# Experts: the activation evaluated twice on ScalarE, into a half-precision and a single-precision buffer, instead of once with a cast on VectorE

## The reference, cut to what matters

```
t = _ln_t(tokens)                       # 6272 tokens of 256 channels
gate_logits = t @ Wg + bg
top_w, top_i = top_k(gate_logits, 2)    # softmax over the two
for e in range(8):
    h = gelu(t @ W1[e] + b1[e])         # 256 -> 1024
    out = out + w_dense[:, e:e + 1] * (h @ W2[e] + b2[e])   # 1024 -> 256
```

## Time and profile before

| | |
|---|---|
| median of three timed runs | 1256.61 us (1252.85 to 1258.9) |
| profiled execution, span | 1258.3 us, mean granted TensorE clock 0.952 |
| TensorE matmuls busy | 1111.1 us, 88% |
| VectorE busy | 880.8 us, 70% |
| ScalarE busy | 621.6 us, 49% |
| GpSimd busy | 727.7 us, 58% |
| experts' activations on ScalarE | 392 of 128x256 and 64 of 128x128 |
| experts' casts and subtractions on VectorE | 424 each, 327 and 461 ns in the mean |

### The profile page before, as it was taken

One profiled execution on the slowest core, in us unless ns is written; L12 is line 12 of the kernel. 1 busy time (PEld: TensorE's weight loads), 2 busy tenths in 40 slices (PEclk: granted clock), 3 DMA queues, 4 the chain that ended last, 5 costly groups with the idle time before them and its releaser, 6 DMA issues. The chain is left out here.

```text
span 1258.3 us, 37927 instructions
## 1 busy us (share of the span) xinstructions
PE 1111.1 (88%) x12025; PEld 947.3 (75%) x12026; DVE 880.8 (70%) x3115; ACT 621.6 (49%) x1315; POOL 727.7 (58%) x786
## 2 busy tenths in 40 slices
PE   4898888989989879972399999999999999999994
PEld 2666678989889868762288888888888888887783
DVE  7887787998989859874366666666676666665452
ACT  4565677988889847651133333333233333333321
POOL 6324255666666617777346566666666666665454
PEclk9999999999999989975699999999999999999998
DMA  7979788778789479986212333223332333323222
GB/s 177 257 232 285 232 216 207 198 192 196 194 197 212 145 238 342 367 293 217 68 28 47 50 43 52 48 48 44 51 51 45 50 44 48 51 48 45 33 40 26
DMA packets 150567, 168.40 MB, mean 134 GB/s; under 512 B 15694, under 2 KB 141694, under 8 KB 150086
## 3 DMA queue, kind: packets, MB, share of 16 engines
q1 hardware_dynamic: 109270, 123.59, 34.7%
q0 software_dynamic: 21984, 31.18, 14.5%
q10 hardware_dynamic: 19232, 12.64, 4.6%
HBM read 107.52 MB, written 64.70 MB: 137 GB/s over the span
## 5 line engine op out<-in xcount | busy, mean ns | idle before, releaser
L1696 ACT ACTIVATE e_gf<-e_ps_h,keep_b 128x256 f32<-128x256 f32 x392 | 185.2, 473 | 366.3 <-PE e_ps_h L1602 366.3
L1602 PE MATMUL e_ps_h<-e_xt,w1s 128*128 128x256 f16 x2352 | 283.3, 276 | 5.1 <-PEq L1594 3.7
L1636 PE MATMUL e_ps_y<-w2s,e_g_hi 128*128 x1696 | 281.9, 273 | 0.0
L1602 PEld LDWEIGHTS e_ps_h<-e_xt,w1s 128*128 x2352 | 217.3, 98 | 64.9 <-issue 33.7
L977 POOL TENSOR_TENSOR b_p<-b_s,b_p 128x392 f16<-128x392 f32 x196 | 178.7, 932 | 96.5 <-DVE b_p L864 82.4
L1636 PE MATMUL e_ps_y<-w2s,e_g_lo 128*128 x848 | 231.8, 273 | 0.0
L1554 POOL DMA_INDIRECT out<-e_y,e_xg x106 | 175.0, 1651 | 83.9 <-POOLq L1549 41.1
L1763 DVE TENSOR_TENSOR e_g_lo<-e_gf,e_g_hi 128x256 f16<-128x256 f32 x424 | 195.3, 461 | 14.6
L1636 PEld LDWEIGHTS e_ps_y<-w2s,e_g_hi 128*128 128x128 f16 x1696 | 164.2, 98 | 18.6
L1761 DVE CAST e_g_hi<-e_gf 128x256 f16<-128x256 f32 x424 | 138.7, 327 | 31.1 <-ACT e_gf L1696 21.3
L923 ACT ACTIVATE b_s<-b_s,b_neg_max 128x196 f32<-128x196 f32 x392 | 159.2, 460 | 0.3 <-DVE b_neg_max L845 0.2
(11 more groups left out here) (174 smaller groups left out, 1643.6 us busy)
## 6 DMA issues: line engine op xcount, KB each, us to landing
h_v<-v_rows SPq DMA_DIRECT2D x196, 99.5 KB
e_xg<-slots SPq DMA_DIRECT2D x49, 273.0 KB, 2.8
a_w_in<-in_w SPq DMA_DIRECT2D x16, 512.0 KB, 4.5
c_w_in<-in_w SPq DMA_DIRECT2D x16, 512.0 KB, 8.7
v_rows<-h_v_sb SPq DMA_DIRECT2D x14, 455.0 KB, 7.0
a_x<-in_x SPq DMA_DIRECT2D x14, 448.0 KB, 6.2
qk_hi<-h_o_hi SPq DMA_DIRECT2D x14, 448.0 KB, 4.8
qk_lo<-h_o_lo SPq DMA_DIRECT2D x14, 448.0 KB, 6.7
```

The lines of the kernel that those rows point to most:

```text
L1602: mm = pe.matmul(ps_h[:, hc % 4, 0:ST], w1s[:, bass.ds(e, 1), w, a:a + 128].rearrange("p a n -> p (a n)"), xt[:, s, :, 2 * p + k, :], star ...
L1636: mm = pe.matmul(ps_y[:, s, h * C:(h + 1) * C], g[:, s, hc, h * 128:(h + 1) * 128], w2s[:, bass.ds(experts[h], 1), w, a:a + C].rearrange(" ...
L1696: act.activation(gf[:, hc % 4, :], ps_h[:, hc % 4, 0:ST], ACT.Gelu, bias=b1_sb[:, bass.ds(e * HC + hc, 1)], scale=1.0 / WSCALE).then_inc(g ...
```

## The change

In each chunk ScalarE evaluates `Gelu` twice from the same bank of `ps_h`: first into `g_hi`, which is f16, and then into `gf`, which is f32. `g_ok` is raised by the second. VectorE's cast is gone, with the semaphore `hi_ok` and its wait; `split` waits for `g_ok` and subtracts. For the paired halves ScalarE does both writes for each half, four activations in a chunk instead of two.

```
-                                last = act.activation(gf[:, hc % 4, h * HT:(h + 1) * HT], ps_h[:, hc % 4, h * HT:(h + 1) * HT],
-                                                      ACT.Gelu, bias=b1_sb[:, bass.ds(e * HC + hc, 1)], scale=1.0 / WSCALE)
+                                lanes = slice(h * HT, (h + 1) * HT)
+                                for dst in (g_hi[:, n % 2, hc, lanes], gf[:, hc % 4, lanes]):
+                                    last = act.activation(dst, ps_h[:, hc % 4, lanes], ACT.Gelu,
+                                                          bias=b1_sb[:, bass.ds(e * HC + hc, 1)], scale=1.0 / WSCALE)
                             last.then_inc(g_ok, 1)
...
                         act.wait_ge(h_ok, n * HC + hc + 1)
-                        act.activation(gf[:, hc % 4, :], ps_h[:, hc % 4, 0:ST], ACT.Gelu,
-                                       bias=b1_sb[:, bass.ds(e * HC + hc, 1)], scale=1.0 / WSCALE).then_inc(g_ok, 1)
+                        for dst in (g_hi[:, n % 2, hc, :], gf[:, hc % 4, :]):
+                            last = act.activation(dst, ps_h[:, hc % 4, 0:ST], ACT.Gelu,
+                                                  bias=b1_sb[:, bass.ds(e * HC + hc, 1)], scale=1.0 / WSCALE)
+                        last.then_inc(g_ok, 1)
...
                 def split(s):
                     for hc in range(HC):
                         dve.wait_ge(g_ok, hc + 1)
-                        dve.tensor_copy(g_hi[:, s, hc, :], gf[:, hc % 4, :]).then_inc(hi_ok, 1)
-                        dve.wait_ge(hi_ok, hc + 1)
                         dve.tensor_tensor(g_lo[:, s, hc, :], gf[:, hc % 4, :], g_hi[:, s, hc, :], ALU.subtract
                                           ).then_inc(gs_ok, 1)
                     dve.sem_inc(g_ok, -HC)
-                    dve.sem_inc(hi_ok, -HC)
```

More of the change, by code:

```diff
@@ L1475, in stage_e @@
         g_ok = sem("e_g_ok")
-        hi_ok = sem("e_hi_ok")
         gs_ok = sem("e_gs_ok")
```

## The result

| | before | after |
|---|---|---|
| median | 1256.74 us (1252.85 to 1259.48, 7 runs) | 1245.66 us (1243.35 to 1251.5, 7 runs) |
| ratio to before, 95% interval | | 0.9917 (0.9894 to 0.994) |
| profiled execution, span | 1258.3 us | 1246.1 us |

The change makes the kernel 0.8% faster (0.6% to 1.1%), 11 us by the medians where 12.2 were forecast. The profiled execution took 1247.95 us, 1.9 over its span.

A forecast was written before the change was run, and what follows sets the result against it. TensorE was taken to bound the experts' stage, with 17.3 us of waits for VectorE. A gain of 12.6 less 0.4 for the opening tile took 1256.6 to 1244.4 us; own range 1240 to 1249, 8-in-10 range 1240 to 1254.

The forecast's parts named there:

- The stall and its cause: Full tiles' up matmuls: TensorE waits for VectorE's cast and subtraction, 17.3 us over 47 tiles.
- Rival B: Experts' stage: TensorE starts late because of its own sequencer, so no change, 1255 to 1258 us; chance 8%.
- The distance of two activations: ScalarE in each chunk: a second activation starts 0.371 us after the first, bounds 0.36 to 0.47.
- The stall that is left: Full tiles after the change: 0.10 us a tile (0.07 to 0.14), so a gain of 12.6 us.
- up parts of 5.31 to 5.38: Sign of being right: us from first up matmul to the transposes, in nearly all tiles, instead of 5.66.
- 7p - 2.56: Chunk 7's lateness in us, p being the distance of two activations; 0.04 at p = 0.371.
- The opening tile: TensorE's stop before tile 1: ScalarE falls behind and delays the operand copy, costing 0.4 us once.
- The halves, the end of the split, the tail: Four paired-half tiles: no cost, 2 us if cover fails; split ends at 7.45 instead of 7.48; tail follows last activation.
- The sum: Whole kernel: -12.6 + 0.4 = -12.2 us, from a median of 1256.6 to 1244.4.
- C: Full tiles: ScalarE becomes the bound and the kernel slower, 1276 us at p = 0.47; chance 8%.
- D: Full tiles: GpSimd's `e_y` holds up VectorE's subtraction, 0.5 us or more a tile, 1268 us or more; chance 4%.
- Subtractions of more than 0.6: Sign of being wrong: VectorE's subtractions in the experts' stage taking over 0.6 us.

The follow-up runs named there:

- the second trace: The changed kernel run once more without further edits, against the kernel before: 1248.66 us, ratio 0.9931.

## Why the prediction was right, point by point

- **The stall and its cause.** The forecast read 17.3 us of waits from six rows; summed over the 47 tiles the trace of before has 15.2 + 2.0 = 17.2. That the two agree so closely is in part luck. The forecast gave 0.42 to 37 tiles and 0.18 to ten; in the up parts 21 tiles lose 0.36 or more (most of them 0.39 or 0.40), 17 lose 0.24 to 0.34, and nine 0.13 to 0.20, which is 15.2. The other 2.0 are waits before the transposes, 1.4 of them in three tiles, and are not VectorE's. That the 15.2 are VectorE's cast with its wait is shown by the runs: 0.1 us with the cast gone and ScalarE's single pass as before, 21.6 with both passes and the cast kept, 38.9 with a third activation. Rival B, TensorE's sequencer, has fallen.
- **The distance of two activations.** 0.371 was taken; the starts are 0.357 apart in a train, and the subtractions behind them 0.73 a pair, 0.365 each. An f16 output costs nothing extra. The Trainium skill's figures (ScalarE: Activation LUTs, "What ACT_TABLE_LOAD costs"), from which the estimate of 0.40 came, are too high for this kernel.
- **The stall that is left.** 47 x 0.10 = 4.7 us were forecast. The two traces after have 1.2 + 4.6 and 1.9 + 2.2, that is 5.8 and 4.1. The sum fits, but its parts do not: in the up parts it is 0.03 to 0.04 a tile and not 0.07 to 0.14, and the up parts of 5.31 to 5.38 that were to be seen in nearly all tiles are seen in three and in eight of 46; most are shorter. Two terms were off. The distance of two activations weighs seven times in the forecast's own formula for the last chunk, 7p - 2.56: with 0.364, by the ends, it gives nothing where 0.371 gave 0.04. And the subtractions under `e_y` took 0.50 and 0.42 instead of 0.58 and 0.57, so chunks 4 and 5 had room to spare. The rest are waits before the transposes, of which the forecast had 0.02 a tile in its 0.42 and nothing in the new stall. That they fill the gap is luck.
- **The opening tile.** Forecast +0.4. TensorE's stop before tile 1 is 2.93 at 626.63 where it was 2.51, which is it. The up parts of the two opening tiles were 0.6 shorter in this trace and 0.2 longer in the second one, so it does not show in the span.
- **The halves, the end of the split, the tail.** In the four tiles of halves the up parts together are 0.3 to 0.4 us shorter than before, so the four activations a chunk cost nothing there. VectorE's last subtraction ends at 7.35 after the first matmul (forecast 7.45). From the end of TensorE's last matmul to the end of the span it is 16.9 us before and 16.7 after, so the tail is the same.
- **The sum.** 1256.6 - 12.2 = 1244.4 was forecast, and 1245.66 and 1248.66 were measured. The second is some 4 us over it, and the single runs of this kernel lie up to 9 us apart. By the medians of the kernels run side by side the gain is 11.1 and 9.1 us; by the experts' stage in the traces it is 11.9 and 11.3, close to the 12.2.
- **Rivals C and D.** C did not happen, and the third activation shows that it was close. D, a whole `e_y` of delay, did not happen: the longest of the 424 subtractions after the change took 0.67 us, 0.24 over the usual 0.43, and in the second trace 0.69. Subtractions of more than 0.6, which the forecast had named as a sign of being wrong, are two in the first trace and 15 in the second; they are too few to cost more than the 1.2 and 1.9 us above. The Trainium skill's rule (SBUF — State Buffer, "SBUF: two separate sides"), by which one of the two engines stands still for the other's whole instruction, is not borne out by these rows.

## What to carry to other kernels

When the busiest engine reads 99.7% busy, compare the starts of equal pieces of its work before calling it the bound: here two parts of a tile with the same matmuls took 5.24 and 5.66 us, and most of the difference, 15.2 us or 1.2% of the kernel in all, belonged to an engine that was busy for 63% of the stretch. To move work from a late engine to one with time to spare, price it by the distance of two starts, not by the length of one, and follow the chunks one by one through the ring: what counts is how far the new pace falls behind before the last chunk that has to wait. Then see what margin is left; a fifth of a microsecond a chunk separated this gain from twice as large a loss. And where the rest of the program varies by as much as the gain, measure the changed stage by itself.

## What the runs showed of the hardware that I had not expected

- In a train of activations the starts stand 0.357 us apart, but each one's duration in the profile grows, from 0.47 to 0.58 over sixteen (872.78 and 877.77 above) and to 0.65 in the longer train with the third activation. The ends are 0.364 apart, and VectorE follows the ends. A mean of 0.52 us in the page's groups is therefore no sign that the operation itself has become slower.
- VectorE and GpSimd slow each other, but who pays changes. With VectorE busy without a pause, its operations under `e_y` lost 0.11 to 0.16 each, and the two `e_y` took 1.91. After the change, in the tile shown, two of three subtractions lost nothing, and the two `e_y` took 2.10; over the trace, 88 of the 130 subtractions that lie under an `e_y` for 0.2 us or more took 0.44 or less, where it was 13 of 101 before. It is not the pauses between the subtractions that spare them: with the third activation these are longer (0.35), and still the two subtractions under `e_y` took 0.58 and 0.56, and the `e_y` 1.83. What decides is open.
- In the kernel before, `e_y` starting 0.16 us earlier went with 3.7 us less of TensorE's waits in the up parts of 47 tiles. That the shift of two engines' operations against each other is the cause is read from the rows above, not separated by a run of its own.
